# Gated two-layer block: probabilities turned by VectorE, products with values in eight array tiles

## The chip, the cores and the metric

The kernel runs on one core of a Trainium2 chip. The metric is device time in microseconds (us) of one execution; lower is better. The engines are TensorE (PE in the profile, PEld for its weight loads), VectorE (DVE), ScalarE (ACT), GpSimd (POOL) and SyncE (SP), which here only issues transfers.

## The reference

Two layers run one after the other on x (2 batches x 512 tokens x 128) with a context of 77 rows per batch. Layer 0 is a cross-attention with 8 heads of 64 and a feed-forward with quantised weights and activations; layer 1 is an attention with 16 heads of 8 over the context and a mixture of 8 experts. Each result is added to x behind the tanh of a gate. The change is in layer 0's attention, whose core is:

```python
kv_input = jnp.concatenate([xn, ln], axis=-2)     # 512 + 77 = 589 keys
kv = kv_input @ Wkv
k, v = jnp.split(kv, 2, axis=-1)
q, k, v = (heads(q), heads(k), heads(v))          # 8 heads of 64
q = q / scale
sim = jnp.einsum('bhid,bhjd->bhij', q, k)
attn = jax.nn.softmax(sim, axis=-1)
out = jnp.einsum('bhij,bhjd->bhid', attn, v)
return out.transpose(0, 2, 1, 3).reshape(B, L, H * dh) @ Wout
```

All of it is float32. Softmax divides each row of exponentials by its sum, before or after the product with the values.

## The kernel before, in words

The work is cut into items, listed by `items()` and named by letters. For each batch: `x0` normalised and turned tokens, `v` values, `q` and `k` queries and keys of a pair of heads (4 pairs), `u` one score tile of 128 queries x 589 keys of one head (32 per batch, 64 in all), `w` the product of probabilities and values of a pair of heads and half of the queries (8 per batch), `o` the output projection, `n` the next normalisation; `f1` to `f4` are the feed-forward, `a1` to `a6` the second attention (`a4` its scores), `m1` to `m4` the experts.

The order of the work is written out: the string `PLAN` is a list of words `item:stage`. `orders()` turns it into one fixed order per engine: F and B are stages on TensorE, A on ScalarE, D on VectorE, P on GpSimd, Ca and Cd a copy by ScalarE or VectorE. The digit behind F is the PSUM bank (of 8) that the item takes; wide items take two. A suffix such as `+22@6` puts 22 turns of the identity into bank 6 ahead of the item; PLAN has 86 of them, 8 ahead of the first `k` and 78 behind the first attention. Each engine walks its order strictly, waiting on semaphores where another engine's result is needed, so a late item holds back everything behind it on its engine.

The life of a `u` (before): TensorE makes the scores (L602, L603), VectorE the negated row maximum (L1063), ScalarE the exponentials with their sum into one of three buffers PR (L842, RING is 3). TensorE turns the 589 columns in five transposes of up to 128 (L535) into the same PSUM banks, and ScalarE (L777, 34 times) or VectorE (L779, 30 times) copies 128x640 to PT. The banks are free after that copy.

The life of a `w` (before): VectorE inverts the sums of four `u` (L1039), GpSimd spreads the reciprocals over 64 columns per head (L495), TensorE turns them (L535, tile REC) and multiplies values and probabilities in two 128x64 array tiles (L621, ten products, the two heads side by side). ScalarE copies the turned reciprocals out of PSUM (L856) and VectorE multiplies (L1070) into OT, which `o` projects (L628).

Lines L778 and on are the helper that copies; L535 is the helper `turn`, which all transposes share; so groups are told apart by their tiles. In the second attention S1 holds exponentials in a ring of three (L916, L908, L1291), TensorE turns them, and L696 multiplies in four 128x32 tiles. SP issues all large loads and, for each pair of heads, four transfers that double the split keys across the partition halves (`double`); the weights of the feed-forward are loaded behind the first of them.

```python
for c in range(5):
    r = P if c < 4 else C
    for e in range(2):
        h = 2 * p + e
        mm = pe.matmul(W[e * DH0:(e + 1) * DH0, 0:N], V[0:r, c, h * DH0:(h + 1) * DH0],
                       PT[0:r, s, c, e, :], start=(c == 0), stop=(c == 4))
```

## Time and profile before

| | before |
|---|---|
| device time, median of 3 runs | 274.52 us (273.43 to 274.93) |
| the profiled execution's own time | not listed beside its profile |
| its span, first to last instruction | 271.8 us |
| TensorE / its weight loads busy | 250.7 us (92%) / 185.5 us (68%) |
| VectorE / ScalarE / GpSimd busy | 230.8 (85%) / 184.1 (68%) / 32.4 us (12%) |
| data moved | 10.70 MB in 8848 packets |
| granted TensorE clock | full |

Busy time is the time in which an engine has at least one instruction in work; matmuls are pipelined and their ends are modelled. A line such as L535 can be that of a helper. A group line says how many instructions it has, their summed busy time, the mean duration of one in ns, and how long the engine was idle just before them and for whom. Instructions of one engine can overlap, so a row of the timeline with x20 is shorter than twenty means.

### The profile page before, as it was taken

The page shows a single profiled execution, that of the slowest core. Times are in us where ns is not written, and L with a number is a line of the kernel's source. Part 1 is how long each engine was busy: PE and PEld are TensorE (multiplying, and loading weights), DVE is VectorE, ACT ScalarE, POOL GpSimd, SP SyncE. Part 2 cuts the span into 40 slices and gives each one's busy share as a digit, 9 for nine tenths or more (in the row PEclk, how much of TensorE's full clock was granted, in tenths as well). Part 3 has the DMA queues.
Part 4 walks back from the last instruction along what each step waited for, and adds up shares of the span by engine and source line. Part 5 has one row for each costly group of instructions (what it writes and reads, how often), then busy time and mean ns, then how long its engine had stood idle before and what let it go on. Part 6 is the DMA issues. An engine that isn't in the chain of part 4 may idle for free.

```text
span 271.8 us, 5455 instructions
## 1 busy us (share of the span) xinstructions
PE 250.7 (92%) x1772; PEld 185.5 (68%) x1772; DVE 230.8 (85%) x561; ACT 184.1 (68%) x462; POOL 32.4 (12%) x57
## 2 busy tenths in 40 slices
PE   0999999999999999999999999978868999999996
PEld 0767687787688866677688878755545665757665
DVE  5699969886679976999989789899999999998781
ACT  2596669776577557768879862159799596773561
POOL 3100000000001010000000021320002302133230
PEclk9999999999999999999999999999999999999999
DMA  7198620030300003300300000000000000000001
GB/s 205 38 251 309 151 53 2 0 91 0 91 0 1 4 0 89 91 0 4 89 0 4 0 2 0 4 0 0 4 0 2 2 0 4 0 10 4 29 0 41
DMA packets 8848, 10.70 MB, mean 39 GB/s; under 512 B 1115, under 2 KB 5877, under 8 KB 8821
## 3 DMA queue, kind: packets, MB, share of 16 engines
q1 hardware_dynamic: 7792, 9.70, 13.4%
q10 hardware_dynamic: 1029, 0.65, 0.8%
q8 instruction: 15, 0.25, 0.4%
q14 instruction: 12, 0.10, 0.1%
HBM read 4.99 MB, written 0.52 MB: 20 GB/s over the span
## 4 chain that ended last, share of the span: by engine, by line
PE 62%; DVE 23%; issue 7%; ACT 6%; DMA 1%; DVEq 0%; ACTq 0%
PE slot L535 18%; PE slot L621 11%; PE slot L602 6%; PE slot L603 5%; PE slot L580 3%; PE slot L762 3%; PE slot L628 2%; PE slot L586 2%; DVE nm L1063 2%; ACT S L916 2%; DVE mx L1172 2%; ACT PR L842 2%; PE slot L756 2%; PE slot L592 1%; PE slot L713 1%
## 5 line engine op out<-in xcount | busy, mean ns | idle before, releaser
L842 ACT ACTIVATE PR<-slot,nm 128x589 f32<-128x589 f32 x64 | 47.6, 750 | 14.8 <-DVE nm L1063 12.5
L1063 DVE TENSOR_REDUCE nm<-slot 128x1 f32<-128x589 f32 x64 | 46.4, 763 | 3.6 <-PE slot L603 3.2
L535 PE MATMUL slot<-K,PR 128*128 128x128 f32 (+1 forms) x320 | 44.4, 278 | 1.7 <-ACT PR L842 1.5
L535 PEld LDWEIGHTS slot<-K,PR 128*128 128x128 f32 (+1 forms) x320 | 35.5, 142 | 12.3 <-ACT PR L842 10.2
L602 PE MATMUL slot<-KH,Q 128*128 128x296 f32 (+1 forms) x128 | 40.7, 336 | 0.8 <-DVE PT L779 0.4
L621 PE MATMUL slot<-PT,V 128*64 128x256 f32 (+1 forms) x320 | 38.1, 384 | 0.0
L603 PE MATMUL slot<-KL,Q 128*128 128x296 f32 (+1 forms) x128 | 36.1, 299 | 0.0
L621 PEld LDWEIGHTS slot<-PT,V 128*64 128x64 f32 (+1 forms) x320 | 21.6, 137 | 11.9 <-issue 2.7
L602 PEld LDWEIGHTS slot<-KH,Q 128*128 128x128 f32 x128 | 24.1, 188 | 5.6 <-issue 2.1
L777 ACT ACTIVATE PT<-slot 128x640 f32<-128x640 f32 x34 | 23.5, 705 | 6.4 <-PE slot L535 5.8
L779 DVE COPY PT<-slot 128x640 f32<-128x640 f32 x30 | 24.4, 820 | 2.6 <-PE slot L535 2.3
L603 PEld LDWEIGHTS slot<-KL,Q 128*128 128x128 f32 x128 | 24.3, 190 | 0.5 <-issue 0.5
L495 POOL COPY REC<-rec 128x256 f32<-128x256 f32 x16 | 6.4, 402 | 124.1 <-DVE rec L1039 119.4
L916 ACT ACTIVATE S<-slot,mx 128x77 f32<-128x77 f32 x64 | 19.8, 345 | 0.9 <-DVE mx L1170 0.5
L479 POOL TENSOR_TENSOR vex<-vex,mhalf 128x2 f32<-128x2 f32 (+1 forms) x15 | 10.8, 723 | 49.3 <-DVE vex L998 49.3
L535 PE MATMUL slot<-K,S 128*128 128x128 f32 x80 | 11.7, 281 | 3.9 <-ACT S L916 3.4
L916 ACT ACTIVATION_READ_ACCUMULATOR S<-slot,mx 128x1 f32 x64 | 14.5, 226 | 0.0
L1057 DVE TENSOR_TENSOR KL<-slot,KH 64x590 fp32r<-64x590 f32 x16 | 12.3, 767 | 2.1 <-ACT KH L871 1.8
L1070 DVE TENSOR_TENSOR OT<-slot,RB 128x256 f32<-128x256 f32 x16 | 6.7, 420 | 8.4 <-ACT RB L856 6.0
L535 PEld LDWEIGHTS slot<-K,S 128*128 128x128 f32 x80 | 8.6, 140 | 7.3 <-ACT S L916 5.8
L856 ACT ACTIVATE RB<-slot 128x256 f32<-128x256 f32 x16 | 6.2, 384 | 10.9 <-PE slot L621 10.7
L535 PE MATMUL slot<-K 128*128 128x128 f32 x86 | 12.0, 290 | 1.5 <-ACT PT L791 0.8
(170 smaller groups left out, 502.2 us busy)
## 6 DMA issues: line engine op xcount, KB each, us to landing
KH<-KH SPq DMA_DIRECT2D x16, 147.5 KB, 2.5
KL<-KL SPq DMA_DIRECT2D x16, 147.5 KB, 2.5
CTT<-in_ctxT SPq DMA_DIRECT2D x1, 640.0 KB, 7.1
K<-in_const SPq DMA_DIRECT2D x1, 589.0 KB, 8.1
WGU<-in_wgu SPq DMA_DIRECT2D x1, 580.0 KB, 8.6
out<-X SPq DMA_DIRECT2D x8, 64.0 KB, 1.5
L1W<-in_l1w SPq DMA_DIRECT2D x1, 384.0 KB, 3.4
WD<-in_wdT SPq DMA_DIRECT2D x1, 320.0 KB, 10.8
```

What stands on the lines that cost most here:

```text
L479: pool.tensor_tensor(vex[:, n, r], vex[:, n, r], mhalf[:, r], ALU.pow).then_inc(rstd_ready[n], 1)
L535: return pe.transpose(dst, src, ident[0:p, 0:p])
L580: mm = pe.matmul(W[0:w, n * 512:n * 512 + 512], LT[:, b, c * P:c * P + w], WV[:], start=True, stop=True)
L602: pe.matmul(W[:, K0 + lo:K0 + hi], q, KH[:, g % 4, lo:hi], start=True, stop=False)
L603: mm = pe.matmul(W[:, K0 + lo:K0 + hi], q, KL[:, g % 4, lo:hi], start=False, stop=True)
L621: mm = pe.matmul(W[e * DH0:(e + 1) * DH0, 0:N], V[0:r, c, h * DH0:(h + 1) * DH0], PT[0:r, s, c, e, :], start=(c == 0), stop=(c == 4))
L777: engine.activation(dst, src, ACT.Copy).then_inc(pt_copied["ACT"], 1)
L779: engine.tensor_copy(dst, src).then_inc(pt_copied["DVE"], 1)
L842: act.activation(PR[:, s, :], W[:, K0:K0 + KEYS0], ACT.Exp, bias=nm0[:, s:s + 1], accum_out=sum0[:, b, p * 2 + f, t, e:e + 1]).then_inc(pr ...
L916: act.activation(S1[:, s, j * C:(j + 1) * C], W[:, at:at + C], ACT.Exp, bias=mx1[:, s, j:j + 1], accum_out=sum1[:, b * QT + t, j:j + 1]).t ...
L1057: dve.tensor_tensor(KL[r, s, :], W[r, K0:K0 + KEVEN], KH[r, s, :].bitcast(F32), ALU.subtract).then_inc(k_ready, 1)
L1063: dve.tensor_reduce(nm0[:, s:s + 1], W[:, K0:K0 + KEYS0], AX.X, ALU.max, negate=True).then_inc(max_ready, 1)
```

## The change

- GpSimd multiplies each probability tile by the reciprocals of its row sums, in place in PR. The reciprocals come from VectorE, for two `u` at a time (stage u:D2, 32 in all). The spreading, turning and copying of reciprocals and the multiplication behind the product are gone.
- VectorE turns each probability tile (u:D4) in blocks of 32x32, from PR to PT, 128x608 with padding. TensorE's five transposes per `u` and the copies from PSUM are gone; a score tile's banks are free once the exponentials are made. PR has four buffers.
- After block turns each group of 32 partitions holds its own 32 queries of each tile, so `w` multiplies in eight 32x64 array tiles (4 groups x 2 heads), 19 key blocks long, for all 512 queries of a pair: 8 `w` instead of 16, each over four banks. The results are copied to OT by ScalarE.
- The values must lie in each of the four partition groups: a new `spread` on SP stores V to memory once per batch and loads it, per pair of heads, into V4, four times over, behind a wait for the `w` two before.
- S1 becomes the same buffer as PR (four buffers in the second attention also), PT1 shares PT, HM shares V4, with waits for the last readers.
- PLAN is new; it has no turns of the identity. All copies of PT1 and of quantised tiles are ScalarE's (VectorE had 2 of each).

```diff
+TILE = 32
+KB = -(-KEYS0 // TILE)
+KT = KB * TILE
+GRP = P // TILE
+QB32 = QT * TILE
...
-RING = 3
+RING = 4
...
-        out += [("w", b, p, f) for p in range(NP0) for f in range(2)] + [("o", b, t) for t in range(QT)] + [("n", b, p) for p in range(PARTS)]
+        out += [("w", b, p) for p in range(NP0)] + [("o", b, t) for t in range(QT)] + [("n", b, p) for p in range(PARTS)]
...
-x0:F0 x0:A1 k:F2+8@2 x0:D2 q:F4 k:A1 k:F0 q:A1 k:D1 v:F6 x0:P2 k:A1 q:D1 v:F2 v:Ca k:D1 q:F5 v:Ca u:F6 x0:D3
-q:A1 u:F2 u:F0 u:D1 v:F4 u:D1 u:A1 u:D1 u:A1 u:B v:Cd u:A1 u:B u:Cd q:F4 u:Ca q:D1 u:F6 u:F2 u:D1 u:B u:D1
...
+x0:F6 x0:A1 k:F2 v:F6 k:A1 x0:D2 v:F0 v:F4 k:D1 v:Ca v:Cd v:Ca x0:P2 q:F2 k:F0 q:A1 x0:D3 k:A1 q:D1 k:D1 q:F5 u:F6 q:A1 u:D1
+u:F2 u:A1 u:D1 q:D1 u:F0 u:F6 u:D1 u:F4 u:A1 u:A1 u:D2 u:D1 u:P1 u:P1 u:A1 u:D4 u:D1 u:D2 u:P1 u:A1 u:F0 u:D4 u:F2 u:D1
+u:P1 u:A1 u:D4 x0:F4 u:D1 x0:A1 u:D2 u:D4 u:A1 u:P1 u:F0 u:D1 k:F4 u:A1 s:D2 u:D2 u:D4 q:F6 u:P1 k:A1 u:F0 u:D4 q:A1 u:P1
...
-        PR = sb("PR", [P, RING, KEYS0])
-        PT = sb("PT", [P, 2, 5, 2, N])
-        REC = sb("REC", [P, TP, 2, DH0])
-        RB = sb("RB", [P, 2, N])
+        V4 = sb("V4", [P, 2, KB + 1, 2 * DH0])
+        PR = sb("PR", [P, RING, KP1])
+        PT = sb("PT", [P, 2, KB, 2, QB32])
...
-        S1 = sb("S1", [P, RING, KP1])
-        PT1 = sb("PT1", [P, 2, 2 * KC1, N])
+        S1 = PR
+        PT1 = PT[:].rearrange("p s b e q -> p s (b e q)")[:, :, 0:2 * KC1 * N].rearrange("p s (c n) -> p s c n", n=N)
...
-        HM = sb("HM", [P, QT, MT])
+        HM = V4[:, 0].rearrange("p b d -> p (b d)")[:, 0:QT * MT].rearrange("p (t f) -> p t f", f=MT)
...
+            def spread(g):
+                b, p = g // NP0, g % NP0
+                if p == 0:
+                    for by in ("ACT", "DVE"):
+                        sp.wait_ge(v_copied[by], copied(("v", b, 2), by))
+                    sp.wait_ge(v_pad, 1)
+                    sp.dma_start(VD[b, 0:4 * P].rearrange("(c p) d -> p c d", p=P), V[:, 0:4, :]).then_inc(v_stored, 16)
+                    sp.dma_start(VD[b, 4 * P:KT], V[0:KT - 4 * P, 4, :]).then_inc(v_stored, 16)
+                sp.wait_ge(v_stored, 32 * (b + 1))
+                if g >= 2:
+                    sp.wait_ge(front_done, NTH[KINDS["w"][g - 2]] + 1)
+                vd = VD[b].rearrange("(c i) d -> i c d", i=TILE)[:, :, p * P:(p + 1) * P]
+                for a in range(GRP):
+                    sp.dma_start(V4[a * TILE:(a + 1) * TILE, g % 2, 0:KB, :], vd).then_inc(v_spread[g % 2], 16)
...
+            spread(0)
...
-                if kind == "w":
-                    pool.wait_ge(sum_inverted, n)
-                    if n > 1:
-                        pool.wait_ge(front_done, NTH[KINDS["w"][n - 2]] + 1)
-                    rec = rec0[:, b, item[2] * 2 + item[3]]
-                    pool.tensor_copy(REC[:], rec.unsqueeze(3).broadcast_to([P, TP, 2, DH0])).then_inc(rec_ready, 1)
+                if kind == "u":
+                    _, b, p, f, t, e = item
+                    pool.wait_ge(sum_inverted, (n + 1) // 2)
+                    pr = PR[:, (n - 1) % RING, 0:KEYS0]
+                    pool.tensor_scalar(pr, pr, rec0[:, b, p * 2 + f, t, e:e + 1], None, ALU.mult).then_inc(prob_scaled, 1)
...
-                    _, b, p, f = item
-                    n = upto(item)
-                    s = half_pair(item) % 2
-                    pe.wait_ge(rec_ready, n)
-                    for t in range(TP):
-                        turn(W[:, N + t * P:N + (t + 1) * P], REC[:, t].rearrange("p e d -> p (e d)"))
-                    last = ("u", b, p, f, TP - 1, 1)
-                    pe.wait_ge(v_copied["ACT"], copied(("v", b, 2), "ACT"))
-                    pe.wait_ge(v_copied["DVE"], copied(("v", b, 2), "DVE"))
-                    pe.wait_ge(pt_copied["ACT"], copied(last, "ACT"))
-                    pe.wait_ge(pt_copied["DVE"], copied(last, "DVE"))
-                    for c in range(5):
-                        r = P if c < 4 else C
-                        for e in range(2):
-                            h = 2 * p + e
-                            mm = pe.matmul(W[e * DH0:(e + 1) * DH0, 0:N], V[0:r, c, h * DH0:(h + 1) * DH0],
-                                           PT[0:r, s, c, e, :], start=(c == 0), stop=(c == 4))
+                    g = pair(item)
+                    s = g % 2
+                    pe.wait_ge(v_spread[s], 16 * GRP * (g // 2 + 1))
+                    pe.wait_ge(prob_turned, 8 * (g + 1))
+                    for c in range(KB):
+                        for a in range(GRP):
+                            rows = slice(a * TILE, (a + 1) * TILE)
+                            for e in range(2):
+                                r = slice(e * DH0, (e + 1) * DH0)
+                                mm = pe.matmul(W[r, a * 512:a * 512 + QB32], V4[rows, s, c, r], PT[rows, s, c, e, :],
+                                               start=(c == 0), stop=(c == KB - 1))
...
-                if kind == "u":
-                    pe.wait_ge(prob_ready, n)
-                    for c in range(5):
-                        w = P if c < 4 else C
-                        mm = turn(W[0:w, c * P:(c + 1) * P], PR[:, (n - 1) % RING, c * P:c * P + w])
-                    mm.then_inc(prob_turned, 1)
-                elif kind == "f4":
...
-        def copy_turned(engine, by, item):
-            _, b, p, f, t, e = item
-            n, g = upto(item), half_pair(item)
-            engine.wait_ge(prob_turned, n)
-            if g >= 2:
-                engine.wait_ge(front_done, NTH[KINDS["w"][g - 2]] + 1)
-            dst, src = PT[:, g % 2, :, e, t * P:(t + 1) * P], slot(item)[:, 0:KP].rearrange("p (c q) -> p c q", c=5)
+        def copy_heads(engine, by, item):
+            _, b, p = item
+            engine.wait_ge(front_done, NTH[item] + 1)
+            if b == 1:
+                engine.wait_ge(front_done, NTH["o", 0, QT - 1] + 1)
+            dst = OT[:, p, :].rearrange("p (t a q) -> p a t q", a=GRP, q=TILE)
+            src = slot(item).rearrange("p (a c) -> p a c", a=GRP)[:, :, 0:QB32].rearrange("p a (t q) -> p a t q", q=TILE)
...
-            if part >= 2:
-                engine.wait_ge(front_done, NTH[KINDS["a6"][part - 2]] + 1)
+            former = KINDS["a6"][part - 2] if part >= 2 else ("w", B - 1, NP0 - 2 + part)
+            engine.wait_ge(front_done, NTH[former] + 1)
...
+                    else:
+                        act.wait_ge(prob_turned, len(KINDS["u"]) - RING + n)
...
-                elif kind == "w":
-                    if n > 2:
-                        act.wait_ge(ot_ready, n - 2)
-                    act.activation(RB[:, n % 2, :], W[:, N:2 * N], ACT.Copy).then_inc(rb_ready, 1)
...
-                    _, b, p, f = item
-                    dve.wait_ge(rb_ready, n)
-                    if b == 1:
-                        dve.wait_ge(front_done, NTH["o", 0, QT - 1] + 1)
-                    dve.tensor_tensor(OT[:, p, f * N:(f + 1) * N], W[:, 0:N], RB[:, n % 2, :],
-                                      ALU.mult).then_inc(ot_ready, 1)
...
-                _, b, p, f = item
-                dve.wait_ge(prob_ready, 4 * n)
-                dve.reciprocal(rec0[:, b, p * 2 + f], sum0[:, b, p * 2 + f]).then_inc(sum_inverted, 1)
...
+                if kind == "u":
+                    _, b, p, f, t, e = item
+                    dve.wait_ge(prob_ready, n)
+                    dve.reciprocal(rec0[:, b, p * 2 + f, t], sum0[:, b, p * 2 + f, t]).then_inc(sum_inverted, 1)
...
+            def turn(item):
+                _, b, p, f, t, e = item
+                n, g = upto(item), pair(item)
+                dve.wait_ge(prob_scaled, n)
+                dve.wait_ge(s1_pad, 1)
+                if g >= 2:
+                    dve.wait_ge(front_done, NTH[KINDS["w"][g - 2]] + 1)
+                at = (f * TP + t) * TILE
+                dve.transpose(PT[:, g % 2, :, e, at:at + TILE], PR[:, (n - 1) % RING, 0:KT]).then_inc(prob_turned, 1)
```

## Rows read from the trace of the kernel before

**Rows 1.** The page, parts 1 and 2: busy us (share of the span); granted clock.

```profile
PE 250.7 (92%) x1772; PEld 185.5 (68%) x1772; DVE 230.8 (85%) x561; ACT 184.1 (68%) x462; POOL 32.4 (12%) x57
...
PEclk9999999999999999999999999999999999999999
```

**Rows 2.** By stretch: us; busy PE, PEld, DVE, ACT, POOL; clock, DMA share, GB/s.

```profile
0.00:15.00 15.00, 8.50 (x30) 5.90 (x31) 9.59 (x36) 6.44 (x10) 3.57 (x11) 1.00 0.48 132
15.00:173.00 158.00, 155.31 (x1137) 121.05 (x1136) 135.52 (x283) 111.93 (x232) 10.77 (x23) 1.00 0.19 51
173.00:250.00 77.00, 67.64 (x506) 45.49 (x506) 72.24 (x201) 56.77 (x200) 13.19 (x19) 1.00 0.01 2
250.00:272.00 22.00, 19.21 (x105) 13.10 (x104) 13.42 (x45) 8.98 (x21) 4.83 (x5) 1.00 0.08 22
```

**Rows 3.** VectorE's waits, 15 to 173 us: us in total, times, longest.

```profile
DVE OT L1070 <- ACT RB L856: 6.0, 6, 1.9
DVE nm L1063 <- PE slot L603: 3.2, 6, 1.4
DVE rec L1039 <- ACT PR L842: 2.5, 4, 1.0
```

**Rows 4.** Groups by line and shape: xcount, busy us, mean ns, idle before.

```profile
L621 PE MATMUL slot<-PT,V 128*64 128x256 f32 (+1 forms) x320 | 38.1, 384 | 0.0
...
L779 DVE COPY PT<-slot 128x640 f32<-128x640 f32 x30 | 24.4, 820 | 2.6 <-PE slot L535 2.3
...
L777 ACT ACTIVATE PT<-slot 128x640 f32<-128x640 f32 x34 | 23.5, 705 | 6.4 <-PE slot L535 5.8
...
L1070 DVE TENSOR_TENSOR OT<-slot,RB 128x256 f32<-128x256 f32 x16 | 6.7, 420 | 8.4 <-ACT RB L856 6.0 <-PE slot L621 1.6 <-issue 0.8
...
L495 POOL COPY REC<-rec 128x256 f32<-128x256 f32 x16 | 6.4, 402 | 124.1 <-DVE rec L1039 119.4 <-PE slot L621 4.7
...
L856 ACT ACTIVATE RB<-slot 128x256 f32<-128x256 f32 x16 | 6.2, 384 | 10.9 <-PE slot L621 10.7
...
L1039 DVE RECIPROCAL rec<-sum 128x4 f32<-128x4 f32 x16 | 2.8, 174 | 2.7 <-ACT PR L842 2.5
```

**Rows 5.** Timeline, 60 to 66 us: start, us, instructions.

```profile
60.78 1.45 DVE L1063 TENSOR_REDUCE nm<-slot 128x1 f32<-128x589 f32 x2 [0.26 <-PE slot L603]
...
61.13 0.38 PE L535 MATMUL slot<-K,REC 128*128 128x128 f32 x2
61.44 2.38 PE L621 MATMUL slot<-PT,V 128*64 128x256 f32 x20
63.75 1.31 PE L535 MATMUL slot<-K,PR 128*128 128x128 f32 x10
```

**Rows 6.** Timeline, second attention's products, whole and cut off at 204.1 us.

```profile
204.07 1.50 PE L696 MATMUL slot<-PT,V 128*32 128x256 f32 x24
...
204.07 0.42 PE L696 MATMUL slot<-PT,V 128*32 128x256 f32 x4
```

**Rows 7.** Timeline, second attention's first scores (32-row tiles).

```profile
173.92 0.80 PE L681 MATMUL slot<-KBD,Q 32*128 32x308 f32 x8
```

**Rows 8.** Groups by shape, as rows 4.

```profile
L523 POOL TENSOR_TENSOR HM<-HM,cwt 128x512 f32<-128x512 f32 x8 | 8.3, 1045 | 23.0 <-ACT HM L939 15.4 <-DVE cwt L1254 7.6
...
L1291 DVE TENSOR_REDUCE sum<-S 128x8 f32<-128x616 f32 x8 | 6.1, 779 | 0.0
...
L1092 DVE TENSOR_SCALAR W<-W 128x512 f32<-128x512 f32 x2 | 0.8, 423 | 0.0
```

**Rows 9.** Stretch 0 to 30 us; the page's DMA issues.

```profile
0.00:30.00 30.00, 23.01 (x110) 16.18 (x110) 24.05 (x61) 18.51 (x34) 3.97 (x12) 1.00 0.69 202
...
KH<-KH SPq DMA_DIRECT2D x16, 147.5 KB, 2.5
```

**Rows 10.** VectorE's first reader of the feed-forward weights.

```profile
L1216 DVE TENSOR_REDUCE ws<-W x1: 676/676/676, 25.2 to 25.2; 128x1 f32<-128x512 f32 x1
```

**Rows 11.** Turns on the identity alone.

```profile
L535 PE MATMUL slot<-K 128*128 128x128 f32 x86 | 12.0, 290 | 1.5 <-ACT PT L791 0.8 <-DVE YC L1116 0.6
```

More of the change, by code:

```diff
@@ L203, in sem @@
             return stack.enter_context(nc.semaphore(name))
[L205 removed]
+        PS = stack.enter_context(nc.psum_tensor("PS", [P, BANKS * 512], F32))
         X = sb("X", [P, NT, D])
@@ L461, in _ @@
                 double(g)
+                spread(g)
             ov = out.rearrange("(t p) d -> t p d", p=P)
```

160 lines of the change are left out of this document (79 added, 81 removed).

## The prediction, made before the changed kernel was run

> **What bounds the kernel now.** I read the page's busy shares first [rows 1]: TensorE 92%, VectorE 85%, ScalarE 68%, GpSimd 12%, the granted clock full in every slice (2.4 GHz, the higher of its two levels). Shares are averages, so I cut the span into four stretches [rows 2]: a start (0 to 15 us), the first attention with batch 0's feed-forward (15 to 173), the second attention with batch 1's feed-forward (173 to 250), the end (250 to 272). The change lies in the second. There TensorE is busy 155.3 of 158 us (98.3%), VectorE 135.5 (86%), ScalarE 111.9. VectorE's idle time there has named causes [rows 3]: most of it is the normalisation of one product `w` waiting for ScalarE's copy of the reciprocals, or maxima waiting for scores. TensorE waits for nearly nothing. So the stretch is TensorE's, with VectorE 20 us behind it. In the third stretch VectorE is the fuller one (72.2 of 77, 94%); the end is a chain of short steps.
>
> The page gives a span of 271.8 us. The profiled execution's own time is not listed; the three runs have a median of 274.52, 2.7 above the span, and I add 2.7 to every span below. A measurement of this kernel can tell about 0.5% (1.4 us) from no change.
>
> **TensorE, what goes.** Each of 64 probability tiles is turned by five transposes: ten in a row take 1.31 us, the last one 0.27 of it, so they start 0.116 us apart [rows 5], 64 x 5 x 0.116 = 37.1 us. Each of 16 `w` turns its reciprocals first, 0.31 us from the first turn to the first product, 5.0 in all. Its products take 2.31 us until the next work starts [rows 5], 37.0 in all. Together 79 us.
>
> **TensorE, what comes.** Eight `w`, each 19 key blocks x 4 row groups x 2 heads = 152 products of 32x64 weights and 128 columns. The 160 float32 products of before stand as 320 records [rows 4], so each new `w` has 304 matmuls and as many weight loads, and all eight `w` 4,864 instructions. Do eight tiles run at once? The trace shows parts of it: two 64-column tiles (L621: 20 in 2.38 us, which is 10 steps of about 0.22), four 32-column tiles, all started between 204.07 and 204.1 us [rows 6], and four 32-row tiles, eight matmuls of 308 columns, two on each tile, in 0.80 in all [rows 7]. Eight at once are in no row. If they do, a step has half of L621's columns, 0.108 us, and 38 steps take 4.1 us; with 0.2 us of entry 4.3, and 35 for eight. The other bound is the closest packing of instructions that lasts: 24 matmuls and 24 loads start within 1.50 - 0.38 = 1.12 us [rows 6], 23 ns each, though there the columns may set the pace. 608 x 0.023 = 14.0 us for one `w`, 112 for eight. I take 4.3, since the tiles in [rows 6, 7] start far closer together than 23 ns whenever the array is free; 14.0 stays in the range. TensorE's path is then 155 - 79 + 35 = 111 us of 158: it stops being the bound.
>
> The Trainium skill (TensorE: Matmul & The Clock Gate, "Wait — 56ns, not 53.3ns?") says that matmuls never start less than about 25 ns apart, however small. By that a `w` would take 304 x 25 ns = 7.6 us. That is near rival (a)'s milder price and would give its time. Four starts within 0.03 us [rows 6] are closer than that, so the trace leaves the rule only longer series; its part of (a)'s chance is 0.08.
>
> **VectorE, what goes.** Neighbours overlap: two maxima of 0.763 take 1.45 together [rows 5], so an instruction occupies its duration less 0.08. 30 copies x 0.74 = 22.2; 16 normalisations x 0.34 = 5.4; 16 reciprocals x 0.17 = 2.8 [rows 4]. Together 30.4.
>
> **VectorE, what comes.** 32 reciprocals x 0.17 = 5.4 (they are shorter, at the same fixed cost). 64 block transposes of 128x608 from SBUF to SBUF. Before has none, so I bound one: below by the one-input SBUF operations, 128x512 in 0.42 [rows 8], in proportion 0.50; above by the copy of 640 columns from PSUM, 0.82 [rows 4]. The nearest row is the reduction of 616 columns out of SBUF, 0.779 [rows 8]; I take 0.77, occupying 0.69: 64 x 0.69 = 44.2. The low bound would take 17 us off, the high one adds 3. Net: 135.5 - 30.4 + 5.4 + 44.2 = 154.7 us of work for a stretch of 158.
>
> The Trainium skill (VectorE: DVE Perf Modes, "The three transpose paths") gives 311 ns for 128x128 bf16. With one column per cycle at its 0.96 GHz for the other 480 that is an estimate of 0.81 us, which would add 2.6 us; no row here shows it.
>
> **ScalarE** loses 34 copies (0.705) and 16 of reciprocals (0.384), 30 us, and gains eight of 128x512, at most 0.705 each, the time of 640 columns [rows 4]: 112 to 88, no bound. **GpSimd** swaps 16 copies of 0.40 [rows 4] for 64 scalings of 128x589. The copy of 256 columns (0.40) and the two-input product of 512 (1.05) [rows 8] give, in proportion to 589 columns, 0.92 and 1.20; a scaling has one input, so I take 0.9, 58 us of 158. It costs nothing while hidden: the new order puts two or more VectorE steps (over 1.4 us) between a reciprocal and its transposes. Without that cover each scaling would add its 0.9.
>
> **Queues.** SP gets, per pair of heads, four transfers of 32 x 19 pieces of 512 B, 1.25 MB, and per batch a store of V. The start moved 202 GB/s [rows 9], so a pair's take about 6 us; they leave when the `w` two before is done and are due a pair (about 20 us) later. The doubling of the next pair's keys (2.5 us) [rows 9] is queued behind their wait, and its scores come after that `w` in TensorE's order. The weights for the feed-forward stand behind the first spread, a few us later than before; their first reader was at 25.2 us [rows 10] and is ordered later now. All zero. Batch 1's values wait for the store, one transfer, hidden by the scores of pair 4.
>
> **The sum.** How full can VectorE be? The third stretch shows 94%, TensorE in this one 98.3%: 154.7 of work takes 157 to 165 us. With four probability buffers instead of three, and half of the waits of [rows 3] gone with the normalisation, I take 97%: 159.5, +1.5. Behind it VectorE loses two copies of probabilities (0.74) and two of quantised tiles (0.34): -2.2 where it is the bound; the 78 idle turns that leave TensorE in this part are cheap, since it is not the bound. Span 271.8 + 1.5 - 2.2 = 271.1, time 273.8. The case's own range is 268 to 280: 94% and the transpose at 0.82 above, a full VectorE and a tighter end below. The 80 us lifted off TensorE buy nothing because 24 us of VectorE's idle time are filled by turning.
>
> **Rivals.**
> (a) TensorE cannot be fed. One mechanism: in a `w`, instruction starts or loads pace the tiles. A `w` holds half of PSUM, so beside it VectorE has two score tiles and the transposes in hand, about 5 us of work; from a `w` longer than that the excess stalls VectorE. If only four tiles run at once, as in [rows 6, 7], a `w` takes 8.4 us: 3.4 too long, less the two score tiles that TensorE has ready (1.4 of maxima), 8 x 2.0 = 16, time 290. At 14.0: 155 - 79 + 112 = 188 against 158, time 304. For: no row has eight tiles, nor more than 48 instructions close together. Against: the starts in [rows 6, 7]. Slower, chance 0.23 (0.15 at 290, 0.08 at 304).
> (b) VectorE waits for GpSimd. The chain exponential, reciprocal, scaling, transpose is three handovers long and a buffer is held through it. If half of the 64 transposes come 0.3 us late: +10, time 284. For: the waits of [rows 3] are of this kind. Against: 1.4 us of cover. Chance 0.07.
> (c) VectorE is filled to 99%, or the transpose runs faster than the reduction, and the deeper ring shortens the second attention: 154.7 / 0.99 = 156.3, -1.7, and -4 behind: time 266 to 268. Chance 0.08.
> (d) The clock falls. 86 turns on the identity (12.0 us) [rows 11] go, and behind 173 us TensorE was busy 67.6 of 77 with most of them. If it is granted 1.2 GHz there for 10 us, products on the chain take twice as long: +5, time 279. Chance 0.04.
>
> **Chances.** The forecast has 0.58: its middle is 0.7 us under the median, so I split it 0.29 faster by over 0.5%, 0.14 within, 0.15 slower. With (c) faster is 0.37; with 0.01 of (b) same is 0.15; (a), (d) and the rest of (b) make slower 0.48. The range 266 to 293 holds the forecast, (b), (c), (d) and the milder half of (a); it leaves out about 0.15 to 0.2.
>
> **What would show it.** Right: VectorE busier than 95% between 15 and 173 us and TensorE under 80%; about 4.3 us per `w`; 0.77 per transpose; VectorE's waits for GpSimd under 5 us in sum. Wrong: a `w` of 7 us or more with idle VectorE behind it (a); transposes that wait for the scaling (b); transposes of 0.5 us or well under 154 us of VectorE's work (c); a granted clock under full anywhere after the start (d).

## The result, and the profile after the change

The changed kernel takes **320.3 us** (median of 4 runs, 319.1 to 323.2) against 274.6 for the kernel before: ratio 1.169, 95% interval 1.165 to 1.173. The forecast was 273.8, the range ended at 293. The profiled execution took 321.2 us, its span is 319.2.

The page of the changed kernel, parts 1, 2, 3 and 4 (before: [rows 1]):

```profile
PE 233.8 (73%) x3446; PEld 172.3 (54%) x3446; DVE 253.1 (79%) x591; ACT 164.2 (51%) x424; POOL 140.2 (44%) x106
...
PEclk9999558898999979658976979999958798999999
...
q1 hardware_dynamic: 29040, 22.16, 32.0%
...
q8 instruction: 28, 0.46, 0.6%
...
PE 35%; DVE 26%; issue 14%; POOL 11%; DMA 5%; ACT 4%; SPq 4%; DVEq 0%; ACTq 0%; POOLq 0%
```

No engine is full any more: TensorE fell from 92% to 73% and VectorE from 85% to 79%. The clock falls to half in places. The chain that ended last has all engines in it, and 14% "issue", time in which an engine waited for nothing that the profile shows. Queue q8 carries instructions: its packets went from 15 to 28, each of 16,384 bytes. TensorE's recorded instructions went from 3,827 to 7,163; by 256 to a packet that is 15 and 28 packets, so these packets are TensorE's. Queue 1 moved 22.2 MB; before it was 9.7.

By stretch, the changed kernel (columns as in [rows 2]):

```profile
0.00:15.00 15.00, 7.72 (x16) 4.20 (x17) 7.70 (x33) 4.60 (x6) 4.19 (x12) 1.00 0.45 127
15.00:213.00 198.00, 137.57 (x2869) 108.59 (x2867) 156.04 (x303) 91.27 (x193) 117.09 (x69) 0.85 0.49 105
213.00:297.00 84.00, 69.28 (x451) 45.56 (x452) 75.19 (x207) 58.58 (x201) 14.16 (x20) 0.90 0.01 3
297.00:319.00 22.00, 19.28 (x114) 13.90 (x112) 14.13 (x50) 9.79 (x24) 4.79 (x5) 1.00 0.07 19
```

The last `w` ends at 213 us, where before it ended near 169: 44 of the 47 us that the span grew lie ahead of it; the work behind it took 3.6 us longer than before (106.4 against 102.8). **VectorE's work there came out as forecast**, 156.0 us against 154.7. What failed is its filling: 156 us of work took 198 us, 79% where I had taken 97%. GpSimd is busy for 117 us there, where it had 11 before and I had added 58.

The groups that carry the change, with what ended the idle time before them (page, part 5; before: [rows 4]):

```profile
L513 POOL TENSOR_SCALAR PR<-PR,rec 128x589 f32<-128x589 f32 x64 | 113.6, 1791 | 77.6 <-DVE rec L1207 77.6
...
L1327 DVE STREAM_TRANSPOSE PT<-PR 128x608 f32<-128x608 f32 x64 | 51.0, 803 | 16.3 <-POOL PR L513 15.9
L1064 DVE TENSOR_REDUCE nm<-PS 128x1 f32<-128x589 f32 x64 | 47.6, 755 | 16.5 <-PE PS L621 15.9
L633 PE MATMUL PS<-PT,V 32*64 32x128 f32 x2432 | 44.1, 291 | 18.9 <-issue 13.8
L633 PEld LDWEIGHTS PS<-PT,V 32*64 32x64 f32 x2432 | 39.5, 141 | 23.7 <-issue 17.8
```

Three things are to be seen. A scaling takes 1.79 us, not 0.9. VectorE waits 15.9 us for scalings, in its transposes (L1327), and 15.9 us for scores, in its maxima (L1064). And the products (L633) have 18.9 us of idle time in front of them, 13.8 of it ended by nothing that shows.

The first `w`, TensorE's weight loads in the timeline (start, us, count, idle before):

```profile
49.59 1.62 PEld L633 LDWEIGHTS PS<-PT,V 32*64 32x64 f32 x109 [0.37 <-ACT PR L851]
53.51 2.84 PEld L633 LDWEIGHTS PS<-PT,V 32*64 32x64 f32 x128 [2.29 <-issue]
57.24 1.24 PEld L633 LDWEIGHTS PS<-PT,V 32*64 32x64 f32 x67 [0.89 <-issue]
```

109 loads, a stop of 2.3 us, 128 loads, a stop of 0.9, 67 loads. With each load goes one matmul, so between two stops lie exactly 256 instructions. I numbered TensorE's records through the trace: every one of the ten stops inside a `w` falls on a multiple of 256 plus the same 193. From its first load to the start of its last matmul the eight `w` last 8.82, 7.65, 5.93, 6.70, 5.74, 6.81, 5.71 and 7.88 us, 55.2 in all against the 35 of the forecast.

From there I had three theories. **A**: the start is late because SP's queue stands at the store of values. **B**: VectorE waits for GpSimd's scaling. **C**: in a `w`, TensorE is paced by the supply of its instructions in blocks of 256.

TensorE also waits once for the doubling of keys, at the ninth scores:

```profile
PE PS L620 <- DMA KL<-KL: 7.5, 1, 7.5
```

### The profile page after: what moved, and what is told of

Read it like the earlier page. It is cut to its first block, busy times and chain, and to the rows that moved or that the text cites. A ratio compares the mean times of both kernels' runs of the same rounds, so it can differ in the third digit from the quotient of the medians.

```text
span 319.2 us, 8855 instructions
## 1 busy us (share of the span) xinstructions
PE 233.8 (73%) x3446; PEld 172.3 (54%) x3446; DVE 253.1 (79%) x591; ACT 164.2 (51%) x424; POOL 140.2 (44%) x106
## 4 chain that ended last, share of the span: by engine, by line
PE 35%; DVE 26%; issue 14%; POOL 11%; DMA 5%; ACT 4%; SPq 4%; DVEq 0%; ACTq 0%; POOLq 0%
PE PS L633 12%; POOL PR L513 11%; PE PS L553 4%; DVE nm L1064 4%; PE PS L620 3%; DMA KL<-KL 3%; PE PS L621 2%; DVE PT L1327 2%; PE PS L769 2%; PE PS L598 2%; PE PS L726 2%; ACT PR L923 2%; DMA values<-V 1%; PE PS L694 1%; PE PS L709 1%
## 5 line engine op out<-in xcount | busy, mean ns | idle before, releaser
L513 POOL TENSOR_SCALAR PR<-PR,rec 128x589 f32<-128x589 f32 x64 | 113.6, 1791 | 77.6 <-DVE rec L1207 77.6
L851 ACT ACTIVATE PR<-PS,nm 128x589 f32<-128x589 f32 x64 | 48.0, 752 | 57.5 <-DVE nm L1064 48.4
L620 PE MATMUL PS<-KH,Q 128*128 128x296 f32 (+1 forms) x128 | 48.3, 388 | 28.4 <-ACT PR L851 13.3
L1327 DVE STREAM_TRANSPOSE PT<-PR 128x608 f32<-128x608 f32 x64 | 51.0, 803 | 16.3 <-POOL PR L513 15.9
L1064 DVE TENSOR_REDUCE nm<-PS 128x1 f32<-128x589 f32 x64 | 47.6, 755 | 16.5 <-PE PS L621 15.9
L633 PE MATMUL PS<-PT,V 32*64 32x128 f32 x2432 | 44.1, 291 | 18.9 <-issue 13.8
L633 PEld LDWEIGHTS PS<-PT,V 32*64 32x64 f32 x2432 | 39.5, 141 | 23.7 <-issue 17.8
L620 PEld LDWEIGHTS PS<-KH,Q 128*128 128x128 f32 x128 | 29.1, 227 | 40.3 <-ACT PR L851 19.9
L621 PE MATMUL PS<-KL,Q 128*128 128x296 f32 (+1 forms) x128 | 42.4, 342 | 0.0
L621 PEld LDWEIGHTS PS<-KL,Q 128*128 128x128 f32 x128 | 29.6, 231 | 2.5 <-issue 2.4
```

The lines of the kernel that those rows point to most:

```text
L513: pool.tensor_scalar(pr, pr, rec0[:, b, p * 2 + f, t, e:e + 1], None, ALU.mult).then_inc(prob_scaled, 1)
L620: pe.matmul(W[:, K0 + lo:K0 + hi], q, KH[:, g % 4, lo:hi], start=True, stop=False)
L621: mm = pe.matmul(W[:, K0 + lo:K0 + hi], q, KL[:, g % 4, lo:hi], start=False, stop=True)
L633: mm = pe.matmul(W[r, a * 512:a * 512 + QB32], V4[rows, s, c, r], PT[rows, s, c, e, :], start=(c == 0), stop=(c == KB - 1))
L851: act.activation(PR[:, s, 0:KEYS0], W[:, K0:K0 + KEYS0], ACT.Exp, bias=nm0[:, s:s + 1], accum_out=sum0[:, b, p * 2 + f, t, e:e + 1]).then_ ...
L1064: dve.tensor_reduce(nm0[:, s:s + 1], W[:, K0:K0 + KEYS0], AX.X, ALU.max, negate=True).then_inc(max_ready, 1)
```

## Experiments: one suspect at a time

**sp_order** moves the first spread behind the loads and the second doubling.

```diff
             double(0)
-            spread(0)
...
-            for g in range(1, B * NP0):
+            double(1)
+            spread(0)
+            spread(1)
+            for g in range(2, B * NP0):
```

> Only SP's order is changed against the changed kernel: the first spread of the values and the feed-forward loads change places with the second doubling of keys, so SP issues first doubling, loads, second doubling, then both first spreads. In the changed kernel the ninth score tile starts at 43.6 us, behind the doubling that landed then. Theory A (SP's queue costs the start): that tile starts at 31 to 35 us and the whole is 8 to 12 us faster, about 310. Rival (GpSimd paces the start too: the scaling of the eighth tile ends at 39 us, and the rest waits anyway): under 5 us faster.

Measured: 320.6 us, ratio 1.171 (1.165 to 1.178): no gain. The ninth scores came at 34.7 instead of 43.6 us, but the 16th maximum ended at 62 us in both kernels. The first `w` took 12.8 us instead of 8.8, with one stop of 6.3. Theory A alone is wrong; the 9 us were given back at the first `w`.

**scale_32** lets GpSimd scale 32 of the 589 columns.

```diff
-                    pr = PR[:, (n - 1) % RING, 0:KEYS0]
+                    pr = PR[:, (n - 1) % RING, 0:32]
```

> GpSimd scales only the first 32 of the 589 columns of each probability tile; the scaling of the other 557 is left out. In the changed kernel a scaling takes 1.76 us, 64 of them 113 us. Theory B (the length of the scaling holds back VectorE's transposes and, through the ring of four, the scores): one scaling under 0.4 us, VectorE's waits for GpSimd from 15.9 to under 3 us, 15 to 30 us faster than 320. Rival (TensorE's products and their gaps set the pace, GpSimd is beside it): under 6 us faster.

Measured: 311.5 us, ratio 1.135 (1.129 to 1.140), 8.8 less. VectorE's wait for GpSimd is gone, while its wait for scores rises to 24.3. Theory B has the place right, but not the size (15 to 30 us): of the 15.9 us of waits 8.8 are won.

**w_half** takes 10 of 19 key blocks in a `w`: 320 instructions, 9 blocks left out.

```diff
-                    for c in range(KB):
+                    for c in range(10):
```

> Each product w takes 10 of the 19 key blocks; 9 are left out, so it has 320 TensorE instructions instead of 608. In the changed kernel a w takes 6.0 to 9.1 us and stalls of 0.9 to 2.3 us stand in it, always at the same place of a block of 256 instructions. Theory C (instructions arrive in blocks of 256, not faster than about one block in 3.3 us): the stalls in w fall from ten to four or fewer and a w to 3 to 4.5 us; the whole 15 to 30 us faster, since each w sits in front of the next scores. Rival (w is not on the path, VectorE and GpSimd are): under 8 us faster.

Measured: 307.5 us, ratio 1.119 (1.113 to 1.125), 12.8 less, under the 15 to 30 of Theory C and over the 8 of its rival. VectorE's wait for scores falls from 15.9 to 7.6 us. Five stops are left of ten. The third `w` meets none:

```profile
87.19 2.31 PEld L633 LDWEIGHTS PS<-PT,V 32*64 32x64 f32 x160 [1.48 <-ACT PR L851]
```

Its 320 instructions take 2.3 us, 14 ns for a load and its matmul: eight tiles do run at once. Products whose instructions are there cost what the forecast said (10/19 of 4.1 is 2.2 us).

**bench_tiles** is a kernel of its own: 304 products in eight 32x64 tiles of 128 columns (L230), the same with 32 columns (L238), 152 products on four row tiles (L252).

```diff
+            def eight_narrow():
+                for c in range(38):
+                    for a in range(4):
+                        for e in range(2):
+                            pe.matmul(PS[e * 64:(e + 1) * 64, a * 512:a * 512 + 32],
+                                      F[a * 32:(a + 1) * 32, e * 64:(e + 1) * 64],
+                                      F[a * 32:(a + 1) * 32, 512:544], start=True, stop=True)
```

> A kernel of its own that computes nothing of the reference: TensorE runs series of float32 products after a warm-up, 304 in eight 32x64 tiles with 128 columns, 304 in the same tiles with 32 columns, 152 in four 32-row tiles with 128 columns, and 80 in two 128x64 tiles with 256 columns. Theory C (supply of instructions): the first two series, 1216 instructions each, take the same time, about 16 us, in blocks of 256 instructions of 3.2 to 3.7 us with an idle stretch at the end of each. Rival D (the array or the loads of eight tiles pace it): the first takes 8.2 us or more without idle stretches (76 steps of 0.108) and the second a quarter to a half of it. The last series, 320 instructions, should take its 40 steps of 0.216, 8.6 us, under both.

Its weight loads in the timeline, 128 columns, 32 columns, then four tiles:

```profile
20.87 1.85 PEld L230 LDWEIGHTS PS<-X 32*64 32x64 f32 x128 [1.21 <-issue]
24.88 1.85 PEld L230 LDWEIGHTS PS<-X 32*64 32x64 f32 x128 [2.15 <-issue]
28.60 1.85 PEld L230 LDWEIGHTS PS<-X 32*64 32x64 f32 x128 [1.87 <-issue]
32.06 0.42 PEld L230 LDWEIGHTS PS<-X 32*64 32x64 f32 x24 [1.60 <-issue]
...
38.00 2.28 PEld L238 LDWEIGHTS PS<-X 32*64 32x64 f32 x220 [0.76 <-issue]
42.38 1.92 PEld L238 LDWEIGHTS PS<-X 32*64 32x64 f32 x128 [2.09 <-issue]
46.38 1.92 PEld L238 LDWEIGHTS PS<-X 32*64 32x64 f32 x128 [2.08 <-issue]
...
61.92 8.28 PEld L252 LDWEIGHTS PS<-X 32*64 32x64 f32 x304 [0.76 <-issue]
```

A block of 256 instructions runs in 1.9 us and the next begins 3.5 to 4.0 us after its start, whether a product has 128 columns or 32. So the columns don't set the pace of the blocks. The granted clock was full in the first series and 0.50 (1.2 GHz) in the blocks of the second that are shown between 42 and 54 us; at full clock its first 220 loads took 2.28 us, 10 ns each, against 14 with 128 columns. Inside a block the columns do count. Eight tiles take 1.9 us for 128 loads, four tiles 3.5, so the eight do run at once. The four-tile series takes 8.3 us for its 608 instructions, 3.5 us per 256, and nothing stops.

The instruction packets tell the same directly. Each of the ten stops in the changed kernel ends 1.2 to 1.5 us after a packet of q8 has landed: the first one lands at 52.1 us, and the loads go on at 53.5. In bench_tiles, where the DMA engines are idle, it is 1.2 to 1.6 us. Theory C holds: 3.5 to 4.0 us per 256 instructions is the price here, about 15 ns for each, up to 9.5 us for 608 in a row. A lone `w` costs 5.7 to 8.8 because part of its blocks is already there.

**bf16_values** tests C the other way round, with whole `w`: scaled and turned probabilities and the spread values are bf16, so a product is one matmul, 304 instructions for 19 key blocks.

```diff
-        V = sb("V", [P, 5, IN0])
+        V = sb("V", [P, 5, IN0], BF16)
...
-                    pool.tensor_scalar(pr, pr, rec0[:, b, p * 2 + f, t, e:e + 1], None, ALU.mult).then_inc(prob_scaled, 1)
+                    pool.tensor_scalar(PRB[:, (n - 1) % RING, 0:KEYS0, 1], pr, rec0[:, b, p * 2 + f, t, e:e + 1], None, ALU.mult).then_inc(prob_scaled, 1)
...
-                                mm = pe.matmul(W[r, a * 512:a * 512 + QB32], V4[rows, s, c, r], PT[rows, s, c, e, :],
+                                mm = pe.matmul(W[r, a * 512:a * 512 + QB32], V4B[rows, s, c, r], PTB[rows, s, c, e, 0:QB32],
```

> Scaled probabilities, turned probabilities and the spread values are bf16 instead of float32; all 19 key blocks are kept. A product is then one matmul instead of two: 304 instructions per w instead of 608, at the same 38 steps of columns as the shortened w had 40 instructions' worth fewer; the spreads move 256 B pieces, half the bytes; GpSimd and VectorE do the same counts. Theory C (a w is paced by the supply of instructions): as with the halved w, 320 instructions, -12.8 us, so about 307 us, or less if the transposes of bf16 are quicker than 0.803 us. Rival (a w is paced by its columns, its weight loads or its data): with the same number of products of the same size less than 5 us of gain. It computes with rounded probabilities and values.

Measured: 307.4 us, ratio 1.124 (1.118 to 1.129): the forecast 307 for halved instructions. Its transposes take 805 ns, no less than the float32 ones, its scalings take 1967, and VectorE's wait for them rises to 18.6 us, so neither explains the gain; the halved spreads may have a share in it.

**sp_act** gives the scaling to ScalarE, beside the order of sp_order.

```diff
+                    act.wait_ge(sum_inverted, (n + 1) // 2)
+                    act.activation(pr, pr, ACT.Copy, scale=rec0[:, b, p * 2 + f, t, e:e + 1]).then_inc(prob_scaled, 1)
```

> The whole computation, with the first spread behind the loads and the second doubling, and with the scaling done by ScalarE (Copy with a scale per partition) at the place in the order where GpSimd did it. ScalarE's price for 589 columns should be near its copies, 0.6 to 0.75 us, against GpSimd's 1.76. Theory B (GpSimd's slow scaling costs what its waits show): with the wait of VectorE for GpSimd gone, about 311 us as with the scaling of 32 columns. Rival: the scaling stands on ScalarE ahead of the next exponentials, waits there for the reciprocals and holds back exponentials and maxima: 316 to 325 us.

Measured: 328.7 us, ratio 1.201 (1.195 to 1.207). Its waits:

```profile
DVE nm L1065 <- PE PS L617: 28.3, 14, 9.8
...
ACT PR L957 <- DVE rec L1208: 10.8, 11, 3.2
```

The scaling itself takes 0.78 us, less than half of GpSimd's. But it stands in ScalarE's order in front of exponentials, and VectorE's wait for scores grows from 15.9 to 28.3 us. The rival was right: a shorter instruction at a worse place costs 8 us.

## Experiments: what takes the rest, and do the parts add up

**all_three** puts sp_order, scale_32 and w_half together.

> Three edits at once: the first spread of values behind the loads and the second doubling, GpSimd scales 32 of 589 columns, a w takes 10 of 19 key blocks (the other 9 are left out of the output). Alone they gave 0.3 slower (within the noise), 8.8 and 12.8 us. Theory E (each stands in its own place): they add up, 320.3 - 0 - 8.8 - 12.8 = 298.7 us. Theory F (they hide one another: the 9 us that the order of SP's queue took from the start were given back at the first w because that w was slow): with the short w the start keeps its gain, about 290 us. If these three are all that is wrong with the changed kernel, the time falls to 274 us or less; whatever stays above it has another cause, the granted clock first (Theory G).

Measured: 292.1 us, ratio 1.065 (1.060 to 1.070), nearer to Theory F. But the first `w` takes 9.8 us for its 320 instructions, the third of w_half took 2.3. Its weight loads:

```profile
45.13 2.91 PEld L635 LDWEIGHTS PS<-PT,V 32*64 32x64 f32 x109 [2.08 <-issue]
53.43 1.56 PEld L635 LDWEIGHTS PS<-PT,V 32*64 32x64 f32 x51 [5.40 <-issue]
```

and the DMA engines between 36 and 60 us (packets, MB, share of 16 engines):

```profile
q1 hardware_dynamic: 6745, 3.81, 89.1%
q8 instruction: 2, 0.03, 0.7%
```

The stop of 5.4 us falls where two spreads at once fill the DMA engines. The instruction packet that ends it starts at 50.4 us, 2.4 us after TensorE has stopped. Part of the 9.8 us is the clock: it was 0.50 there, and 109 loads took 2.91 us where the changed kernel's took 1.62 at full clock.

**late_spread** holds the second spread back until the first `w` is done.

```diff
-                if g >= 2:
-                    sp.wait_ge(front_done, NTH[KINDS["w"][g - 2]] + 1)
+                if g >= 1:
+                    sp.wait_ge(front_done, NTH[KINDS["w"][max(g - 2, 0)]] + 1)
```

> The three edits (292.06 us), and the second pair's values are spread only when the first w is done, so that queue 1 is nearly empty while the first w runs. Theory H: the first w (45.2 to 55.0 us instead of 2.3) stood still for 5.4 us because its next block of instructions is fetched by the same DMA engines that were then full with two spreads at once (V<-values x12 between 36 and 60 us). Without the second spread that stretch falls to 2 us or less, the 16th maximum ends by 53 us instead of 58.8, and the time falls by 4 to 6 us, to 286 to 288. Rival (the block is late for another reason): the stretch stays over 4 us and the time at 291 to 293.

Measured: 296.6 us, ratio 1.081 (1.077 to 1.084), 4.6 **more**. The same loads, and TensorE's longest wait between 50 and 80 us:

```profile
43.88 2.91 PEld L635 LDWEIGHTS PS<-PT,V 32*64 32x64 f32 x109 [0.85 <-issue]
47.25 0.97 PEld L635 LDWEIGHTS PS<-PT,V 32*64 32x64 f32 x51 [0.46 <-issue]
```

```profile
PE PS L622 <- DMA KL<-KL: 9.6, 1, 9.6
```

The mechanism is as expected: the instruction packet starts at 44.9 us, while the loads still run, the stop shrinks from 5.4 to 0.5 us, the `w` to 4.3, and the 16th maximum ends at 51 instead of 59 us. The same can be seen at the fourth `w` of w_half, all_three and late_spread. It stops for 3.9 to 4.5 us, where the store of batch 1's values (1.25 MB) is under way. A slow block is no protection then: the one before the changed kernel's first stop took 5.5 us, with the DMA engines full. But SP now stands at the new wait, and the doubling of the third pair's keys stands behind it; the 24th maximum ends at 78 instead of 75. **late_full**, the same two edits on the whole computation, says it again:

> The whole computation of the changed kernel, with the first spread behind the loads and the second doubling (alone: 320.6 us) and the second spread behind the first w. By Theory H the first w loses its 6.3 us stretch and the 9 us that were given back there stay gained in part: 311 to 316 us. Rival: 319 to 322, as with the first edit alone.

Measured: 328.8 us, ratio 1.198 (1.194 to 1.202): 16th maximum at 57 instead of 62, 24th at 88 instead of 82. The expected gain did not come; one queue with too much in it gives back what is taken from it elsewhere.

**w_two** leaves two key blocks per `w`, 64 instructions, beside the other two edits.

> The three edits, but each w takes 2 of 19 key blocks, 64 instructions instead of 320 (17 blocks are left out of the output): w costs next to nothing. If what is left above the kernel before (292.06 against 274) is still the fetch of instructions in w, the time falls by some 2,048 instructions at 15 ns, up to 20 us where all of them are on the path, to 276 to 282. Rival (what is left is VectorE's work and the order of the rest): 286 us or more.

Measured: 288.8 us, ratio 1.051 (1.045 to 1.057), only 3.2 less than all_three, as its rival had it (286 or more). TensorE waits three times for doubled keys, 12.4 us in all. So from 10 key blocks down, with the transfers in the way, the length of `w` hardly counts; from 19 to 10 it had been worth 12.8. **q_first** is late_spread with batch 0's first queries ahead of its values:

> As late_spread, and in the orders of TensorE and ScalarE the first queries stand ahead of the values of batch 0, as they did before the change; the first maxima then end near 18 to 19 us instead of 22.1. If the later start is carried to the end, 3 to 4 us under late_spread; if VectorE or the transfers take it back at the ninth scores, less than 1 us.

Measured: 297.5 us against 296.6, no gain. The edit failed as a test: the first two maxima still ended at 21 to 22 us.

So the transfers came out first. **no_spread** drops the store and all spreads (the products then take a constant for the values); **ns_s32** adds scale_32 to it, **ns_s32_two** adds two key blocks per `w`.

```diff
-                spread(g)
...
+                    if n == 1:
+                        for i in range(2):
+                            pool.memset(V4[:, i], 0.01).then_inc(v_stored, 1)
...
-                    pe.wait_ge(v_spread[s], 16 * GRP * (g // 2 + 1))
+                    pe.wait_ge(v_stored, 2)
```

> The changed kernel without the store and the spreads of values: V4 is set to a constant by GpSimd once (the values are left out of the output), everything else as changed. Theory I (the transfers of the spreads are on the path: they hold up the doubling of keys on SP's queue, for which TensorE waited 7.5 us, and the fetch of instructions): 302 to 310 us, 10 to 18 less than 320.3, the larger part of it before the 16th maximum, and the first w takes 6 to 7 us instead of 8.8. Rival (the transfers are hidden, as the forecast had it at zero): 318 us or more.

> No spreads, and GpSimd scales 32 of 589 columns. If scaling and transfers stand in different places, another 8 to 10 us less than no_spread; if the freed transfers only lay the wait for GpSimd bare, more than 10; if scaling was hidden behind them, under 5. What is left above 274 is then w: with whole w near 290 us.

> No spreads, 32 columns of scaling, and 2 of 19 key blocks per w: of the change are left the block transposes on VectorE, the ring of four, the orders. Theory J (nothing but instructions, scaling and transfers made the kernel slower; VectorE's own work is as the forecast had it): 268 to 276 us, VectorE over 93% busy between 15 and the end of the first attention. Rival (VectorE or the new order is slower by itself): 280 us or more.

Measured, in this order, with what each step takes off:

| kernel | us | off | ratio to before (95%) |
|---|---|---|---|
| changed | 320.3 | | 1.169 (1.165 to 1.173) |
| no_spread | 314.6 | 5.8 | 1.145 (1.138 to 1.152) |
| ns_s32 | 302.1 | 12.4 | 1.101 (1.094 to 1.108) |
| ns_s32_two | 280.9 | 21.3 | 1.024 (1.019 to 1.029) |
| before | 274.6 | 6.3 | |

That is less for the transfers than Theory I said (10 to 18), and more than its rival allowed (318 us or more); as Theory I had it, nearly all of it, 5.4 us, is there by the 16th maximum. The scaling gives more than alone (12.4 against 8.8), so the freed transfers laid the wait for GpSimd bare, but 302 us is not the 290 expected. The last step is 21.3 us for 8 x 544 instructions, 4.9 ns each. It takes away the stops and the products together. No run has whole `w` without stops, so how much of it is the stops alone stays open. Steps depend on their order: with short `w` the transfers are worth 8.0 (w_two, which has them, against ns_s32_two), with whole ones 5.8.

The last of them, by stretch and with VectorE's longest waits between 15 and 163 us:

```profile
15.00:163.00 148.00, 99.97 (x630) 73.69 (x628) 141.58 (x274) 87.23 (x186) 25.32 (x66) 0.82 0.21 55
```

```profile
DVE V L799 <- PE PS L584: 1.9, 1, 1.9
DVE rec L1191 <- ACT PR L835: 1.1, 2, 0.9
```

VectorE is 95.7% full, with under 5 us of named waits, and the last maximum ends at 163 us (before: 162). This is the kernel that the forecast described: bound by VectorE, TensorE at 68%. Theory J is right up to there (over 93% busy), but its time (268 to 276) is not: 280.9 lies at the lower end of its rival's range (280 or more). In the profiled execution 4.3 us of the difference to the kernel before lie behind the last maximum, so it is the part behind the first attention that is slower, not VectorE's work in it.

**ns_s32_two_q** puts the queries first once more, in that kernel.

> As ns_s32_two, with the first queries ahead of the values of batch 0. With the transfers gone the first maxima end 3 to 4 us sooner than in it; if that is carried, 2 to 4 us less; if VectorE's work is what counts, within 1 us.

Measured: 281.8 us against 280.9, within its rival's 1 us; again the first maxima did not come sooner (22.4 us), so the order at the start stays untested.

## Experiments: is the low clock a price?

**warm** puts turns on the identity ahead of score tiles and `w`, as `+3` and `+10` in PLAN.

> The changed kernel with three turns on the identity ahead of each of the 64 score tiles and ten ahead of each w, into banks that the next products overwrite: 272 turns, some 32 us of TensorE at 0.116 each where TensorE idles 55 of 184 us between 30 and 214. Theory G (the low granted clock, 0.57 between 30 and 50 us and 0.73 between 110 and 145, is itself a price on the path): the clock goes to 0.95 or more there and the time falls by over 3 us, to 310 to 317. Rival (the clock only follows the waits): the clock rises too, but the time stays within 1.6 us of 320 or goes up by the turns that stand in front of scores, at most 8 us, since 544 more instructions also cost two more blocks of the fetch.

Measured: 327.2 us, ratio 1.191 (1.186 to 1.196). Its stretches 50 to 80 and 110 to 145 us, from an execution that took 332.2:

```profile
50.00:80.00 30.00, 25.13 (x709) 21.43 (x708) 25.31 (x47) 13.40 (x31) 24.25 (x14) 1.00 0.36 73
...
110.00:145.00 35.00, 24.94 (x411) 21.80 (x409) 22.41 (x52) 11.05 (x23) 14.95 (x10) 0.84 0.68 138
```

The clock rose (0.89 to 1.00, 0.73 to 0.84) and the time too, by 6.9 us; as the stretches are from a longer execution, they show the clock and not the price. **two_tail_turns** and **tail_turns** put eight turns ahead of the 16 score tiles of the second attention alone, in ns_s32_two and in the changed kernel.

> ns_s32_two (280.85 us) with eight turns on the identity ahead of each of the 16 score tiles of the second attention, in the bank that the scores overwrite: 128 turns, some 15 us of TensorE at full clock between 165 and 241 us. Theory G (the low clock there is on the path): the granted clock goes above 0.9 between 187 and 211 and the time falls by 2 to 5 us, to 276 to 279. Rival (the clock follows, or the turns stand on the path as much as they save): within 1 us of 280.85 or above.

> The changed kernel (320.3 us) with the same 128 turns. Theory G: 2 to 5 us less, 315.5 to 318.5. Rival: 319.5 to 325.

Measured: 287.0 us against 280.9, and 326.7 against 320.3: 6 us more in both. The first of these lines is the changed kernel, the second is tail_turns, both from 214 to 240 us:

```profile
214.00:240.00 26.00, 18.68 (x105) 12.79 (x104) 24.61 (x63) 16.17 (x56) 2.12 (x3) 0.84 0.01 1
```

```profile
214.00:240.00 26.00, 21.02 (x144) 15.69 (x144) 22.83 (x60) 14.44 (x48) 2.12 (x3) 1.00 0.01 2
```

The clock is full there and VectorE still does less in the same 26 us. Here a raised clock did not pay for turns that stand on the path. In two_tail_turns the turns did not even raise it where they should: between 187 and 211 us it was 0.58, and 0.72 in ns_s32_two, though TensorE was busy for 21.8 and 19.4 of the 24 us. That run is no test of Theory G. That a fall of the clock costs nothing is not shown by any of them, since none raised it without adding work, and a gain could be hidden under the price of the turns (some 15 us of TensorE).

## Why the prediction was wrong, point by point

**What bounds the kernel** ([rows 1, 2]): right as far as it went. VectorE's work came out at 156.0 for 154.7. The step "taken 97% full" is the one that failed: it was 79%. It nearly holds where nothing else is in the way (95.7% in ns_s32_two). VectorE's idle time in the stretch of before was 22.5 us (158 less 135.5), not the 24 of the forecast's last sentence.

**TensorE, what comes: "38 steps take 4.1 us; with 0.2 us of entry 4.3".** The steps came out right where no fetch is in the way: 2.3 us for 10/19 of a `w`, so eight tiles at once. The term left out is the supply. I had looked at how close instructions start and had asked which of two rates lasts; no row had more than 48 together, and a block has 256. Measured: 6.9 us per `w` in the mean, 55 for eight. The bound of 14.0 from [rows 6] was a fair upper end; the choice of the low one was the mistake. That `w` would cost nothing because TensorE is not the bound was the larger one: TensorE makes no scores while it stands in a `w`, which holds half of PSUM besides, and 4,352 instructions fewer took 21.3 us off. Rival (a) had this place and a cover of 5 us plus 1.4 beside a `w`; by it, 6.9 us would have cost 4 us in all. The cover was not there.

The Trainium skill (TensorE: Matmul & The Clock Gate, "Wait — 56ns, not 53.3ns?") sets at least 25 ns between starts. Within a block the trace does not agree: 128 matmuls in 1.85 us are 14 ns apart. With the stop counted it is 27 to 31 ns (3.5 to 4.0 us per 128), so the rule's 7.6 us per `w` came near for another reason. The Trainium skill (Runtime: NRT & Kernel Launch, "Instruction fetch mechanics") names the blocks of 256 instructions and calls the crossing "mostly hidden". The traces agree where a block takes long enough to execute (3.5 us in the four-tile series, with no stop). Where it took 1.8 to 2.8 us, the crossing cost 0.9 to 2.3 us in the changed kernel.

**GpSimd: "a scaling has one input, so I take 0.9 ... costs nothing while hidden".** It takes 1.79. Against scale_32 (391 ns for 32 columns) that is 1.40 us for 557 more columns, 2.5 ns each; my upper bound of 1.20, by the two-input product in [rows 8], was no bound. VectorE's work beside it is not the cause: 59 of the 64 scalings took 1.76 to 1.77 us, whether VectorE was busy for a third of one or for all of it. With 1.79 us the cover of 1.4 is exceeded by the scaling alone, and rival (b)'s wait came true: 24 times, 15.9 us. Price 8.8 us alone, 12.4 with the transfers gone. I had given (b) 0.07. The Trainium skill (GPSIMD Engine Reference, "4.1 Engine selection") calls operations with one input "roughly line-rate"; 2.5 ns per column against about 1.3 of VectorE (0.779 us for 616 columns, [rows 8]) does not bear that out.

**VectorE, what comes: 0.77 per transpose.** 0.803, between my bounds; the error is 64 x 0.03 = 2 us. The estimate of 0.81 from the Trainium skill (VectorE: DVE Perf Modes, "The three transpose paths") agrees.

**Queues: "All zero".** Wrong by 5.8 to 8.0 us. Two of its sentences failed: that the doubling of keys is queued behind harmless waits (TensorE waited 7.5 us for KL<-KL), and that a spread's traffic is only its own 6 us. It also fills the DMA engines that fetch instructions (a stop of 5.4 us with two spreads at once, 0.5 without).

**The end of the sum: "-2.2 where it is the bound".** The work behind the last `w` took 3.6 us more instead. What it is that costs there was not found.

**(c)** did not happen. **(d)**: its condition came true. The clock fell in more places than I allowed for: it was 0.57 between 30 and 50 us, with TensorE busy for 9.9 of the 15 us before, and 0.90 between 213 and 297 us. The 3.6 us behind the last `w` are near the +5 of (d), but no run shows that the clock is their cause, and none shows that it is not.

**The cases** were taken as rivals of each other, each with its own chance. In fact (a), (b) and the queues came together, and the sum of the three, 39.5 of 45.7 us, lies beyond any one of them. That is why the range missed.

Open are the last 6.3 us. In the profiled execution of ns_s32_two (its span is 5.3 us over that of before), 4.3 lie behind the last maximum, with the clock at 0.87 between 171 and 250 us. The clock, the new order of that part, the ring of four and the copies that moved to ScalarE all stand there together, and none was tried alone.

## What to carry to other kernels

Count an engine's instructions as a resource beside its time: here 256 instructions arrived every 3.1 to 4.1 us, so a long series that executes faster than 12 to 16 ns per instruction is paced by its fetch. Ask what else waits while it stands, here the next scores. That the half of PSUM which it holds matters too was not tested alone. Before pricing work on an engine that "is idle", ask whether its result is on the chain, and take the duration from the same operation, not from a proportion. And where several suspected costs have small chances, ask what happens if all of them are true.

## What the runs showed of the hardware that I had not expected

TensorE stopped at every 256th instruction where the block before it executed in 1.9 us (1.2 to 2.2 us of stop with idle DMA engines, bench_tiles); the stops end 1.2 to 1.6 us after an instruction packet of 16,384 bytes has landed. A block that took 3.5 us had no stop behind it. Under full DMA traffic (89% of 16 engines busy for 24 us) the stop grew to 5.4 us, with the second spread held back it was 0.5. GpSimd's tensor_scalar with a scalar per partition costs 2.5 ns per column at 128 partitions, ScalarE's Copy with a scale 0.78 us for the same 589. VectorE's block transpose of 608 columns takes 0.80 us in float32, and as much in bf16 read from every second element.
